# Logits in a bank of their own, the norm chain two slots earlier, the root behind two scatters: one loop of an audio tower on one core

## What is computed

```python
h = patches(x) @ W + b                                  # 128 x 92 tokens of 128 features
h = h + attention(layernorm(h))                         # 8 heads; the heads' outputs, turned, times Wlt
h = h + mixture(layernorm(h))                           # router over 8 experts, the best 2 of each token

# mixture(t):
gates = softmax(t @ Wr + br)
top_vals, top_idx = top_k(gates, 2); top_vals /= top_vals.sum()
out = sum over e of combine[:, e] * (relu(t @ W1[e] + b1[e]) @ W2[e] + b2[e])
```

## Time and profile before

| | us |
|---|---|
| median of three runs | 1813.76 |
| the profiled execution | 1818.27 |
| its span | 1816.4 |
| PE busy in the span | 1560.2 (86%) |
| DVE busy | 1166.5 (64%) |
| ACT busy | 1050.4 (58%) |
| POOL busy | 767.5 (42%) |

### The profile page before, as it was taken

How to read it: one execution, slowest core, us unless ns; L and a number is a source line. 1 busy time by engine, 2 the same in 40 slices (tenths; PEclk the granted TensorE clock), 3 DMA queues, 4 the chain that set the end, 5 groups by cost and what they waited for, 6 DMA issues and landing times.

```text
span 1816.4 us, 33518 instructions
## 1 busy us (share of the span) xinstructions
PE 1560.2 (86%) x8364; PEld 1258.9 (69%) x8364; DVE 1166.5 (64%) x2839; ACT 1050.4 (58%) x2345; POOL 767.5 (42%) x884
## 2 busy tenths in 40 slices
PE   6689999999999999999878889889668888888840
PEld 4568887888788878887667677767546667666630
DVE  3557888788888888888756665655535555455532
ACT  2457777777777777777645555454334444444410
POOL 1453333333333332333266555555625455455444
PEclk9889999999999999999987887887779999999975
DMA  3312222222222222222375445445246556566558
GB/s 75 105 63 76 79 75 91 75 79 75 91 75 79 75 91 75 79 75 83 134 260 185 157 166 187 168 155 185 69 166 206 199 199 209 194 209 207 189 185 299
DMA packets 144102, 247.31 MB, mean 136 GB/s; under 512 B 23856, under 2 KB 86976, under 8 KB 144064
## 3 DMA queue, kind: packets, MB, share of 16 engines
q1 hardware_dynamic: 112784, 204.37, 32.1%
q0 software_dynamic: 15008, 34.34, 5.6%
q10 hardware_dynamic: 16272, 8.15, 1.6%
HBM read 100.78 MB, written 90.43 MB: 105 GB/s over the span
## 4 chain that ended last, share of the span: by engine, by line
PE 54%; issue 15%; DVE 10%; POOL 9%; DMA 7%; ACT 3%; SPq 2%; another core or an unknown queue 0%; POOLq 0%; DVEq 0%; ACTq 0%
PE bank L308 11%; PE bank L310 9%; PE bank L309 9%; PE bank L1338 6%; PE bank L1400 4%; PE bank L1268 4%; PE bank L1366 3%; DMA w2t<-w2s 2%; POOL y_scratch L691 2%; DMA y_scratch<-ytok,tin 2%; POOL rstdA L565 2%; POOL sorted_scratch L663 1%; DVE aT_l L1060 1%; PE bank L1259 1%; DVE total L1007 1%
## 5 line engine op out<-in xcount | busy, mean ns | idle before, releaser
L558 POOL TENSOR_TENSOR prob<-expo,inv 92x368 f32<-92x368 f32 x256 | 205.0, 801 | 520.7 <-DVE inv L1017 520.7
L691 POOL DMA_INDIRECT y_scratch<-ytok,tin x212 | 202.9, 957 | 231.8 <-DVE ytok L1222 154.8
L1213 DVE SCALAR_TENSOR_TENSOR hid_l<-bank,hid_h 128x512 fp32r<-128x512 f32 x212 | 146.2, 691 | 190.0 <-ACT hid_h L902 119.7
L902 ACT ACTIVATE hid_h<-bank 128x512 fp32r<-128x512 f32 x212 | 126.2, 598 | 205.9 <-PE bank L310 156.9
L663 POOL DMA_INDIRECT sorted_scratch<-trow,posi x184 | 180.7, 982 | 145.2 <-DVE posi L1139 87.4
L1338 PE MATMUL bank<-z,xnT 128*92 128x368 f32 x512 | 203.2, 479 | 0.0
L1060 DVE TENSOR_TENSOR aT_l<-bank,aT_h 128x512 fp32r<-128x512 f32 x184 | 125.8, 691 | 113.0 <-ACT aT_h L839 84.4
L1041 DVE TENSOR_TENSOR w2s<-bank,w2s 128x368 fp32r<-128x368 f32 x256 | 136.8, 534 | 69.6 <-ACT w2s L794 69.6
L1012 DVE TENSOR_REDUCE peak<-bank 92x4 f32<-92x368 f32 x256 | 136.1, 532 | 69.6 <-PE bank L1338 69.4
L839 ACT ACTIVATE aT_h<-bank 128x512 fp32r<-128x512 f32 x184 | 109.0, 598 | 120.7 <-PE bank L1400 118.4
L785 ACT ACTIVATE expo<-cent 92x368 f32<-92x368 f32 x256 | 129.9, 507 | 74.9 <-DVE cent L1022 66.0
(11 more groups left out here) (187 smaller groups left out, 4031.4 us busy)
## 6 DMA issues: line engine op xcount, KB each, us to landing
ax_scratch<-val SPq DMA_DIRECT2D x64, 736.0 KB, 3.7
arow<-ax_scratch SPq DMA_DIRECT2D x23, 2048.0 KB
w2t<-w2s SPq DMA_DIRECT2D x53, 512.0 KB
tin<-sorted_scratch SPq DMA_DIRECT2D x53, 260.0 KB
w1t<-w_h SPq DMA_DIRECT2D x53, 256.0 KB
w1t<-w_l SPq DMA_DIRECT2D x53, 256.0 KB
xin<-in_x_dram SPq DMA_DIRECT2D x32, 372.0 KB
yin<-y_scratch SPq DMA_DIRECT2D x46, 256.0 KB, 4.4
```

Of the source, the lines that this page charges most:

```text
L558: nc.gpsimd.tensor_tensor(prob[:, k % 2], expo[:, k % 2], inv[:, k % 2].unsqueeze(2).to_broadcast([S, HH, S]), ALU.mult).then_inc(prob_kep ...
L691: pool.indirect_dma_start(out=y_dram, out_offset=bass.IndirectOffsetOnAxis(ap=tin[:, b, r, D:D + 1].bitcast(I32), axis=0), in_=ytok[:, b % ...
L1213: V.scalar_tensor_tensor(hid_l[:, f], hid_ps[f][:], 0.0, hid_h[:, f].bitcast(F32), ALU.max, ALU.subtract).then_inc(hidl_kept, 1)
```

## The change

It touches the second part alone:

- The logits get PSUM bank 6 for themselves; the transposed h1 has bank 3 alone. `logits(c)` follows `turn_h(c)` at once in slot 1 and waits for `mask` of the chunk before instead of `posi`. `turn_h(c)` now waits until ACT has read the transposed h1 of chunk c-1 instead of c-2.
- `keep_lean` moves from slot 3 to 1, `keep_res` from 2 to 1, `keep_squares` from 3 and 4 to 2 and 3. `keep_var2` stays in slot 4 but comes ahead of the low half. `keep_trow` is cut in two, in slots 6 and 7.
- POOL issues two scatters ahead of the root and six behind it.
- The rows' names in `trow` are laid once by two iotas and raised in place by 2 x 512 with one instruction a chunk; the tile `goal`, its copy and the wait between are gone.

```diff
--- before.py
+++ after.py
@@ -199,7 +199,6 @@
...
         posi = sb("posi", [P, 2, 2, RT], I32, stack=second)
-        goal = sb("goal", [P, 2, RT], stack=second)
         trow = sb("trow", [P, 2, 2, RT, ROWW], stack=second)
@@ -239,9 +238,9 @@
...
         front_ps, score_ps, probT_ps, mix_ps, val_ps = bank[0:2], bank[2:4], bank[4:6], bank[6], bank[7]
-        turn_ps, proj_ps, tok_ps, res_ps = (bank[0], bank[1], bank[4], bank[7]), bank[2], (bank[3], bank[6]), bank[3]
-        count_ps = bank[5]
-        lg_ps = count_ps[:, 0:RT * (NE + 1)].rearrange("p (r e) -> p r e", r=RT)
+        turn_ps, proj_ps, tok_ps, res_ps = (bank[0], bank[1], bank[4], bank[7]), bank[2], bank[3], bank[3]
+        count_ps, logit_ps = bank[5], bank[6]
+        lg_ps = logit_ps[:, 0:RT * (NE + 1)].rearrange("p (r e) -> p r e", r=RT)
         cum_ps, ntile_ps, row_ps = res_ps[:, 0:NE], res_ps[:, 64:64 + NE], bank[6][0:1, 0:2 * TILES]
@@ -621,13 +620,13 @@
...
                           allow_small_or_imprecise_dtypes=True))
-            lay(pool.iota(goal[:], pattern=[[-T, 2], [1, RT]], base=T, channel_multiplier=RT,
-                          allow_small_or_imprecise_dtypes=True))
             lay(pool.iota(starts[:], pattern=[[0, 1]], base=0, channel_multiplier=TT,
...
                           allow_small_or_imprecise_dtypes=True))
-            lay(pool.memset(trow[:, :, :, :, D:ROWW], 0.0))
+            for half in (0, 1):
+                lay(pool.iota(trow[:, half, :, :, D:D + 1].bitcast(I32), pattern=[[-T, 2], [1, RT]],
+                              base=T + (half - 2) * CT, channel_multiplier=RT))
             lay(pool.memset(trow[:, :, :, :, D - 1:D], 1.0))
@@ -645,21 +644,20 @@
...
-                pool_waits((var2_kept, c + 1), (trow_kept, c - 1), (mask_kept, c - 1))
+                pool_waits((var2_kept, c + 1), (trow_kept, 2 * c - 2), (mask_kept, c - 1))
                 nc.gpsimd.tensor_tensor(rstdB[:, q], varB[:], power[:], ALU.pow).then_inc(rstd2_kept, 1)
...
                 pool_waits((scattered[q], 16 * 2 * RT * (c // 2) if isinstance(c, int) else 8 * 2 * RT * (c - q)))
-                nc.gpsimd.tensor_copy(trow[:, q, :, :, D:D + 1].bitcast(I32), goal[:].unsqueeze(3)).then_inc(goal_kept, 1)
-                pool_waits((goal_kept, LAID + 2 * c + 1))
-                nc.gpsimd.tensor_scalar(goal[:], goal[:], float(CT), None, ALU.add).then_inc(goal_kept, 1)
-
-            def scatter(c, q, choice):
-
-                if choice == 0:
-                    pool_waits((goal_kept, LAID + 2 * c + 2), (trow_kept, c + 1), (posi_kept, c + 1))
-                for r in range(RT):
+                mine = trow[:, q, :, :, D:D + 1].bitcast(I32)
+                nc.gpsimd.tensor_scalar(mine, mine, 2 * CT, None, ALU.add).then_inc(goal_kept, 1)
+
+            def scatter(c, q, first, last):
+
+                if first == 0:
+                    pool_waits((goal_kept, LAID + c + 1), (trow_kept, 2 * c + 2), (posi_kept, c + 1))
+                for choice, r in [(k // RT, k % RT) for k in range(first, last)]:
                     pool.indirect_dma_start(
@@ -668,18 +666,17 @@
...
                 if after_first:
-                    scatter(c - 1, 1 - q, 0)
+                    scatter(c - 1, 1 - q, 0, 2)
                 root2(c, q)
                 if after_first:
-                    scatter(c - 1, 1 - q, 1)
+                    scatter(c - 1, 1 - q, 2, 2 * RT)
                 set_goals(c, q)
...
             steps_second(pool, chunk)
-            for choice in (0, 1):
-                scatter(NCH - 1, (NCH - 1) % 2, choice)
+            scatter(NCH - 1, (NCH - 1) % 2, 0, 2 * RT)
@@ -843,17 +840,17 @@
...
                 for r in range(RT // 2 * half, RT // 2 * (half + 1)):
-                    ins = A(square[:, r], tok_ps[q][:, r * D:(r + 1) * D], ACT.Square, scale=D ** -0.5, bias=lean[:, r:r + 1],
+                    ins = A(square[:, r], tok_ps[:, r * D:(r + 1) * D], ACT.Square, scale=D ** -0.5, bias=lean[:, r:r + 1],
                             accum_out=varB[:, r:r + 1])
...
-            def keep_trow(c, q):
+            def keep_trow(c, q, half):
...
                 act.wait_ge(goal_kept, SETUP)
-                for r in range(RT):
-                    ins = A(trow[:, q, :, r, 0:D - 1], tok_ps[q][:, r * D:(r + 1) * D - 1].unsqueeze(1).to_broadcast([P, 2, D - 1]),
+                for r in range(RT // 2 * half, RT // 2 * (half + 1)):
+                    ins = A(trow[:, q, :, r, 0:D - 1], tok_ps[:, r * D:(r + 1) * D - 1].unsqueeze(1).to_broadcast([P, 2, D - 1]),
                             ACT.Identity, scale=rstdB[:, q, r:r + 1], bias=shift[:, q, r:r + 1])
@@ -862,7 +859,7 @@
...
                 dst = h1tok[:, c * RT:(c + 1) * RT] if isinstance(c, int) else h1tok[:, bass.ds(c * RT, RT)]
-                A(dst, tok_ps[q][:].rearrange("p (r d) -> p r d", r=RT), ACT.Copy).then_inc(res_kept, 1)
+                A(dst, tok_ps[:].rearrange("p (r d) -> p r d", r=RT), ACT.Copy).then_inc(res_kept, 1)
@@ -875,12 +872,13 @@
...
                         keep_aTh(c + 1, j)
-                    if j == 2:
+                    if j == 1:
                         keep_res(c, q)
-                    if j in (3, 4):
-                        keep_squares(c, q, j - 3)
+                    if j in (2, 3):
+                        keep_squares(c, q, j - 2)
+                    if j in (6, 7):
+                        keep_trow(c, q, j - 6)
                     if j == AC - 1:
-                        keep_trow(c, q)
                         keep_gapexp(c)
@@ -1090,7 +1088,7 @@
...
                 step_no[0] = 0
-                at_least(dve, trow_kept, c - 1)
+                at_least(dve, trow_kept, 2 * c - 2)
                 at_least(dve, rstd2_kept, c + 1)
@@ -1150,6 +1148,8 @@
...
                 for j in range(AC):
+                    if j == 4:
+                        keep_var2(c)
                     if more:
@@ -1157,10 +1157,8 @@
...
                         assert step_no[0] == NR, step_no
-                    if j == 3:
+                    if j == 1:
                         keep_lean(c)
-                    if j == 4:
-                        keep_var2(c)
                     if j == 5:
@@ -1411,15 +1409,15 @@
...
                 at_least(pe, h1_kept, c + 1)
-                at_least(pe, trow_kept, c - 1)
-                at_least(pe, res_kept, c - 1)
+                at_least(pe, trow_kept, 2 * c)
+                at_least(pe, res_kept, c)
                 for r in range(RT):
-                    ins = nc.tensor.transpose(tok_ps[q][:, r * D:(r + 1) * D], h1[:, q, r * P:(r + 1) * P], ident[:])
+                    ins = nc.tensor.transpose(tok_ps[:, r * D:(r + 1) * D], h1[:, q, r * P:(r + 1) * P], ident[:])
                 ins.then_inc(res_done, 1)
...
-                at_least(pe, posi_kept, c)
+                at_least(pe, mask_kept, c)
                 for r in range(RT):
@@ -1463,7 +1460,7 @@
...
             pe.wait_ge(holds_kept, 1)
-            pe.wait_ge(trow_kept, NCH)
+            pe.wait_ge(trow_kept, 2 * NCH)
             for k in range(NE):
```

## The result

The kernel with the change takes 1746.8 us (median of 4 runs, 1738.0 to 1759.8) against 1811.2 us (4 runs, 1806.4 to 1817.0) for the kernel before on the same chip: a ratio of 0.965, with a 95% interval of 0.958 to 0.972. The forecast was 1759.

What follows compares the result with a forecast made beforehand. No engine was full: late `shift` and router chain paced chunks, and PE's idles lowered the clock. Terms -46.7 (chunks 4 to 20), -5.5, -2.3, -0.6 made -55: 1763 us profiled, 1759 at the median; range 1738 to 1803.

Steps and rivals of the forecast that it cites:

- `shift` in a full-clock chunk: Second part, DVE: `shift` 8.1 us after h1, then 5.5 to the next h1; 13.6 us a chunk instead of 16.13.
- `lean`, the variances and the root: Full-clock chunk: mean two slots sooner, variances ready 1.2 us sooner, root behind two scatters ending at 1165.35 instead of 1167.86.
- Slow starts at 16.6: Chunks starting at the lower clock, held by ACT's sixth high half: 16.6 us instead of 17.0, gain between 0 and 0.8.
- the logits' new place at 0: PE, logits behind `turn_h`: 0.72 us more in a slow start, covered by PE's idle at chunk end, so 0.
- rival D: Logits ahead of the third turn delay later turns and the sixth high half at the lower clock: +14, 1828 us; chance 0.05.
- Four slow starts of 17: Chunks 4 to 20: as PE's idle before project 6 shrinks, 4 of 17 start at the lower clock instead of 15.
- rival B: The clock goes on falling behind every second chunk, 9 of 17 at 17.0 us: -36 in all, 1777 us; chance 0.21.
- The sum of chunks 4 to 20: Second part: 13 chunks at 13.6 and 4 at 16.6 us, 243.2 instead of 289.9, -46.7.
- Chunks 0 to 3 and chunk 21: Ends of the second part: -5.5 us for chunks 0 to 3, weight splits delaying 2 and 3; -2.3 for chunk 21.
- The tail: After h1 of chunk 22, bound by POOL's 16 scatters and a root: -0.6 us, bounds 0 and -1.6.
- Names in place at 0: POOL, `set_goals`: one small instruction and a wait fewer a chunk, hidden, so 0.
- Rival C: ACT's sixth high half stays late and slow starts stay as they are: -6 to -15, 1799 to 1808 us; chance 0.13.

Runs made afterwards that it cites:

- Experiment 1: The kernel after with the root behind four scatters again, the rest of the change kept: 1812.95 us, ratio 0.9998 against the kernel before.
- experiment 3: The kernel before with six idle matmuls, results unused, ahead of projects 6 and 7 of each chunk: 1782.7 us, ratio 0.9841.
- Experiment 5: The kernel before with only the row names laid once and raised in place: 1814.5 us, ratio 0.9989.
- six later edits, experiments 6 to 8 and 10 to 12: Kernel after with counts one slot later (1805.2 us), also late router links (1818.7; with idle matmuls 1837.5), root behind one scatter (1833.5), earlier weight splits (1798.3; with idle matmuls 1829.6).
- experiments 1 to 5: Kernel after, root behind four scatters (1812.95 us); kernel before, POOL's order alone (1798.3), idle matmuls (1782.7); kernel after, idle matmuls (1739.7); kernel before, names in place (1814.5).
- experiments 5 to 12: Names in place on kernel before (1814.5 us); on kernel after: counts later (1805.2), late links (1818.7, filled 1837.5), root behind three/one scatters (1789.8/1833.5), earlier splits (1798.3, filled 1829.6).
- experiments 1 to 4: Kernel after, root behind four scatters (1812.95 us); kernel before, POOL's order alone (1798.3); kernel before, idle matmuls (1782.7); kernel after, idle matmuls (1739.7).

## Why the prediction was right

The likeliest case came out in its mechanism, 12 us below in time and inside its range. Step by step:

- **`shift` in a full-clock chunk, 8.1 us after h1, chain of 5.5 behind it, 13.6 in all.** Right: 7.94 and 5.21, 13.15 in chunk 8 and 13.24 in the mean, at the lower bound of 13.2 to 14.6. The chain was too dear: 5.46 came from chunk 8 before, where it began late. Of the terms this is the largest error, 13 full-clock chunks x 0.36 = 4.7 us.
- **`lean`, the variances and the root.** `lean` 3.88 us after h1 (3.9 forecast), variances ready 6.37 after (6.3), the root at 6.67 (6.6). DVE had no wait in front of `shift`.
- **Slow starts at 16.6.** Right for chunk 9 (16.36), wrong for chunk 16 (18.13). I had costed the logits' new place at 0, with PE's idle at the end of the chunk as their cover. Where the half clock holds from h1 on, that cover lies on the wrong side: the delay reaches the sixth high half first (11.66 us after h1 in chunk 16, 9.93 in chunk 9). Experiment 1 has it without the rest, 18.0 instead of 16.95. That was rival D, and it was right about the place and the price of about 1 us, wrong about how many chunks would pay it.
- **Four slow starts of 17.** Two, chunks 9 and 16, and chunk 15, which is long without one. Chunks 15 and 16 come of POOL's standstill, for which the prediction had no term, and not of PE's short idles. 0.28 and 1.18 us of idle, as in chunk 8, stand in nearly all full-clock chunks, and the clock fell behind one of them, chunk 8 itself. That the count came out near four is in part luck. The section of the Trainium skill that I weighed ("TensorE: Matmul & The Clock Gate", "A second HAM failure mode: psum-queue depth-cycling") holds for the kernel before, where filling those idles was worth 28 us (experiment 3); it does not say how short an idle must be to do no harm. That shorter idles change nothing, as the prediction and its rival B drew from it, the trace of the kernel after contradicts: 0.94 instead of 0.82.
- **The sum of chunks 4 to 20.** 14 x 13.24 + 51.97 = 237.3 instead of 13 x 13.6 + 4 x 16.6 = 243.2. Fewer and longer such chunks nearly cancel (52.0 for the three long ones, 66.4 for four, less one full-clock chunk of 13.24 = 1.2 us); the chain makes the rest.
- **Chunks 0 to 3 and chunk 21.** -6.3 and -2.9 against -5.5 and -2.3. The weight splits do push the root of chunks 2 and 3: these took 17.28 and 18.20 us.
- **The tail.** -3.3 against -0.6. From h1 of chunk 22 to the end of the last scatter it is 26.7 us before and 25.6 after, -1.1 and within the bounds; the other 2.2 lie between there and the first expert, and no row that I read accounts for them.
- **Names in place at 0.** Experiment 5.
- **The third part within a microsecond or two.** It took 8.9 us less in the profiled execution, without an edit in it; the medians of both kernels differ by 64.4 us, which leaves no room for these 8.9.
- **Rival C** rested on the unexplained 0.41 us. That was a late report of PE, as the trace it was read from has and that of the kernel after has not. It went with the sitting, which I hadn't reckoned with.

What I had no term for are PE's late reports. The same reckoning put six later edits near the kernel after, and they came out 51 to 91 us above it, with waits behind finished matmuls in their traces. Since the kernel after was not run on their chips, this shows neither that the forecast fails for its neighbours nor that it holds for them. What is shown rests on the kernel after and experiments 1 to 5: the mean and the root pay only together, and some half of the gain can be had by keeping the clock up alone.

## What to carry to other kernels

When two waits stand one behind the other on the same chain, price them together: each edit alone gave 0 and 15 us here, both 64. Where PE's clock swings, put matmuls whose result nobody reads into the idle spots once, as a measurement: it tells what is the clock's share (28 us before, some 8 after) before anything is rebuilt. And when an experiment loses time to a wait that no engine's work explains, look for the same wait in a part of the program that wasn't edited, and run the unedited kernel beside it on the same chip, before the loss is laid to the edit.

## What the runs showed of the hardware

- Semaphore increments of PE that land late in the second part, by up to 1.0 us in the mildest trace and 6.4 in the worst, and then several within 0.4 us, in program order, while ACT, DVE and POOL report within 0.02 us (the kernel before and experiments 5 to 12; none in the kernel after and experiments 1 to 4). In experiments 6 to 8 and 10 to 12 the waits behind them cost 2 to 4 us in many chunks, with no busy engine to show for it. Whether they come without the recording is open.
- POOL standing still between two indirect scatters, behind the 113th in each program: 2.14 us before and 4.32 after. Its cause is open.
- Eight matmuls of 128x9 take 0.96 us at the full clock and 1.72 at the half (chunks 8 and 16).
- A part of the program with the same code throughout took 414 to 426 us from one profiled execution to the next, so a difference of 9 us in one pair of profiles is no finding.
